# Fixed expert regions, and routing of three batches inside the attention loop

## The reference, cut to what matters

```
c   = bi_wkv(x, f, f, w1, u1, t)           # gate 1: scans over time, per channel
x1  = x + attention(c)                     # 16 heads of 128, causal, softmax
x2  = bi_wkv(x1, f, f, w2, u2, t)          # gate 2: sigmoid(x1) times a factor f2 that needs f alone
s   = sigmoid(x2 @ gate_w)                 # 32 experts in 4 groups
    keep 2 groups by their maxima, then the 6 best experts; weights = s / sum(s)
out = x1 + sum_k weights_k * expert_k(x2) + (silu(x2 @ sw_gate) * (x2 @ sw_up)) @ sw_down
```

## Time and profile before

| | us |
|---|---|
| median of 3 runs | 2662.51 (2656.43 to 2663.44) |
| the profiled execution | 2666.88 |
| its span, first to last instruction | 2664.7 |
| mean granted clock of TensorE | 0.927 |

### The profile page before, as it was taken

One profiled execution on the slowest core, in us unless ns is written; L12 is line 12 of the kernel. 1 busy time (PEld: TensorE's weight loads), 2 busy tenths in 40 slices (PEclk: granted clock), 3 DMA queues, 4 the chain that ended last, 5 costly groups with the idle time before them and its releaser, 6 DMA issues. The chain is left out here.

```text
span 2664.7 us, 41295 instructions
## 1 busy us (share of the span) xinstructions
PE 2283.1 (86%) x11897; PEld 1923.5 (72%) x11899; DVE 1200.3 (45%) x1953; ACT 1123.1 (42%) x2440; POOL 1425.9 (54%) x993
## 2 busy tenths in 40 slices
PE   1558999999999999998379649999999799999676
PEld 1336888788888887777257428999998789999554
DVE  7335777777755555665452002222222122222355
ACT  2226677676766666666221003233333223333211
POOL 5447766766755555454014754444449976520276
PEclk6678999999999999999779759999999899999788
DMA  1445444644464444431423554444446655422366
GB/s 46 123 139 158 141 140 139 198 140 141 137 203 130 129 130 153 116 117 50 171 79 113 214 189 140 146 144 144 131 149 205 210 182 174 152 90 74 112 200 186
DMA packets 284719, 381.97 MB, mean 143 GB/s; under 512 B 19909, under 2 KB 176649, under 8 KB 280649
## 3 DMA queue, kind: packets, MB, share of 16 engines
q1 hardware_dynamic: 230280, 262.16, 32.7%
q10 hardware_dynamic: 38976, 68.17, 7.6%
q0 software_dynamic: 15360, 50.34, 5.9%
HBM read 247.17 MB, written 133.43 MB: 143 GB/s over the span
## 5 line engine op out<-in xcount | busy, mean ns | idle before, releaser
L1585 POOL TENSOR_TENSOR we_low<-we_raw,we_high 128x1408 fp32r<-128x1408 f32 (+1 forms) x96 | 317.7, 3310 | 8.0
L1583 POOL TENSOR_SCALAR we_high<-we_raw 128x1408 fp32r<-128x1408 f32 (+1 forms) x96 | 135.2, 1408 | 320.5 <-PE up_e L365 315.4
L1693 DVE TENSOR_TENSOR hT_low<-hT_ps,hT_high 128x256 fp32r<-128x256 f32 x127 | 54.0, 425 | 390.2 <-ACT hT_high L1659 390.2
L365 PE MATMUL gate_e<-we_high,xT_high 128*128 x508 | 177.8, 350 | 28.2 <-POOL we_low L1585 27.8
L1706 DVE TENSOR_TENSOR hidden_e<-silu_e,up_e 128x352 f32<-128x352 f32 x127 | 66.2, 521 | 293.1 <-ACT silu_e L1670 293.1
L1670 ACT ACTIVATE silu_e<-gate_e 128x352 f32<-128x352 f32 x127 | 59.0, 465 | 326.3 <-PE up_e L365 326.3
L365 PE MATMUL proj<-c_high,wQ_high 128*128 128x512 f32 x256 | 114.0, 446 | 64.6 <-POOL wQ_low L585 64.6
L1675 ACT ACTIVATE rows_out<-down_e 128x512 f32<-128x512 f32 x127 | 76.0, 599 | 216.5 <-PE down_e L365 216.5
L365 PE MATMUL gate_e<-we_high,xT_low 128*128 x508 | 166.2, 327 | 0.0
L365 PE MATMUL gate_e<-we_low,xT_high 128*128 x508 | 165.9, 327 | 0.0
L365 PE MATMUL up_e<-we_high,xT_high 128*128 x508 | 164.2, 323 | 0.0
(11 more groups left out here) (294 smaller groups left out, 7172.6 us busy)
## 6 DMA issues: line engine op xcount, KB each, us to landing
slots_in<-zero_row SPq DMA_DIRECT2D x80, 416.0 KB
rows_in<-slots_in ACTq DMA_DIRECT2D x129, 256.0 KB, 2.8
slots_out<-rows_out ACTq DMA_DIRECT2D x127, 256.0 KB, 2.1
we_raw<-L_ffn_w_gate SPq DMA_DIRECT2D x32, 704.0 KB, 4.5
we_raw<-L_ffn_w_up SPq DMA_DIRECT2D x32, 704.0 KB, 5.1
w_ring<-L_attn_Wq SPq DMA_DIRECT2D x64, 256.0 KB, 3.6
q_T<-q_out SPq DMA_DIRECT2D x64, 256.0 KB, 2.8
w_ring<-L_attn_Wv SPq DMA_DIRECT2D x64, 256.0 KB, 3.7
```

The lines of the kernel that those rows point to most:

```text
L365: last = nc.tensor.matmul(out, a, b, start=start and i == 0, stop=stop and i == len(terms) - 1)
L1583: nc.gpsimd.tensor_scalar(wh[:, p, at:to], raw[:, at:to], 1.0, 1.0, ALU.mult, ALU.mult).then_inc(w_hi, 1)
L1585: nc.gpsimd.tensor_tensor(wl[:, p, at:to], raw[:, at:to], wh[:, p, at:to].bitcast(F32), ALU.subtract).then_inc(w_split, 1)
L1693: nc.vector.tensor_tensor(htl[:, 0:2, :], psh[:, 0:2 * P].rearrange("p (c t) -> p c t", c=2), hth[:, 0:2, :].bitcast(F32), ALU.subtract)
```

## The change

The slot array gets a fixed region of `CAP` = 2048 + 128 rows for each expert, so a token's slot is the expert's region start plus a running count (`cnt`) that is carried from batch to batch. The rows of a batch are scattered once that batch is routed. The stage after attention

- zeroes 128 rows behind each expert's last row: 32 DMAs whose address SP loads from memory, and one for a region of zeros;
- makes a table with the first row of each of the 127 blocks, which ACT reads for every load of the expert stage;
- makes the packed slots that the combination reads, from slot and expert (`final_slots`).

Batches 0 to 2 are cut in 12 chunks of 128 channels (`chunk_of`), two per iteration from iteration 8 on. A chunk is loaded (x1 and f2), goes through a sigmoid and a product, is split in halves, transposed to rows (`T`), gives its part of the logits (`L`) and is stored both as halves (`x2s`) and as rows. Iterations 10, 12 and 14 choose the experts of batch 0, 1 and 2 (`Z`, `choose`), and iterations 10 to 15 scatter two row tiles each (`z0` to `z3` of POOL, 12 indirect DMAs).

Gate 2 now works on the batch of its own iteration and no longer shares keys with gate 1: it has its own key loads, transposes (`Xy`), copy (`hk`), minima (`hm`) and exponentials (`he`). There are 28 key tiles now, 8 more than before; gate 1 is done after iteration 7. The order strings come in three versions: iterations up to 7, 8 to 11, and 12 to 15 (which have no `Q`). The bias of the output projection is added to x when x is stored.

The stage after attention (`last_route_and_shared_up`) routes batch 3 alone, with x1 still on the chip, loads the halves of the other batches, and has no hardware loops. Only its first column piece (4 items, 8 before) goes over POOL. The expert stage begins with four loads of x1 (`xT`) on SP, ahead of the weights.

```diff
-NBLK_ROOM = NBLK + 3
+CAP = T + P
+ZERO_ROW = E * CAP
-PE_ORDER = "S0 V0 V1 V2 a0 Xx S1 b0 V3 Q0 K2 A0 a1 Q1 b1 S2 K3 A1 Q2 S3 a2 k0 b2 Q3 A2 Xk a3 k1 b3 P0 A3 P1 R0 R1 O2 O3".split()
+PE_ORDER = (
...
+    "S0 V0 V1 V2 a0 S1 V3 b0 Q0 Xy A0 T0 L0 K2 a1 Q1 S2 b1 K3 Q2 Z A1 T1 S3 L1 a2 k0 b2 Q3 A2 a3 k1 b3 P0 A3 P1 R0 R1 O2 O3".split(),
...
+def logit_products(nc, out, c, rt, xh, xl, first, last_one):
+    gwh, gwl = rt["gwh"], rt["gwl"]
+    for t in range(TC):
+        ts = slice(t * P, (t + 1) * P)
+        last = split_products(nc, out[:, t * E:(t + 1) * E], [((xh[:, ts], xl[:, ts]), (gwh[:, c, :], gwl[:, c, :]))], first(t), last_one(t))
+    return last
...
+def send_rows(nc, pool, dr, rt, slot, rows, u, part, parts):
+    for k in range(part * TOPK // parts, (part + 1) * TOPK // parts):
+        pool.indirect_dma_start(dr["xs"], bass.IndirectOffsetOnAxis(ap=slot[:, u, k:k + 1], axis=0), rows, None).then_inc(rt["sent"], 16)
...
+            def send(u, part):
+                if part == 0:
+                    pool.wait_ge(slot_done, u // TC + 1)
+                    pool.wait_ge(rows_in, 16 * (u + 1))
+                send_rows(nc, pool, dr, rt, slot, rowt[:].rearrange("p t c -> p (t c)"), u, part, 2)
...
+            def route_sigmoid(j):
+                act.wait_ge(chunk_in, 32 * (j + 1))
+                nc.scalar.activation(rowst[:], rowst[:], ACT.Sigmoid).then_inc(sig_done, 1)
...
+            sp.dma_start(f2[:], dr["f2"][KC * (B - 1):KC * B].rearrange("k p s -> p k s")).then_inc(f2_in, 16)
+            load_shared(0)
+            load_x2(0)
+            load_x2(1)
+            load_shared(1)
+            load_x2(2)
+            sp.dma_start(dr["x1"][B - 1].rearrange("p (k s) -> p k s", k=KC), x1[:]).then_inc(x1_st, 16)
+            load_shared(2)
+            sp.wait_ge(consts, 3)
+            sp.dma_start(dr["xs"][ZERO_ROW:ZERO_ROW + P, :], zero[:]).then_inc(filled, 16)
+            sp.wait_ge(ends_done, 1)
+            for e in range(E):
+                end = sp.value_load(ends[0:1, e:e + 1], min_val=0, max_val=ZERO_ROW - P)
+                sp.dma_start(dr["xs"][bass.ds(end, P), :], zero[:]).then_inc(filled, 16)
+            for m in range(3, len(SCH)):
+                load_shared(m)
...
+            for i, (m, b) in enumerate(items):
+                n, p = SCH[m][1], i % 2
+                if b == 0 and m + 1 < len(SCH):
+                    split_high(m + 1)
+                act.wait_ge(u_mm, i + 1)
+                wait_hidden(act, i - 2)
+                last = nc.scalar.activation(sg[0:n, p, :], psg[p][0:n, :], ACT.Silu)
...
+            for b in range(B):
+                sp.dma_start(xT[:, b, :, :], dr["x1"][b].rearrange("p (k s) -> p k s", k=KC)).then_inc(x1_in, 16)
             with sp.Fori(0, E) as e:
...
             def load(n, p):
-                act.dma_start(xg[:, p, :], dr["xs"][bass.ds(P * n, P), :]).then_inc(xg_in[p], 16)
+                act.dma_start(xg[:, p, :], dr["xs"][bass.ds(row_of(xrow, n, ZERO_ROW), P), :]).then_inc(xg_in[p], 16)
```

More of the change, by code:

```diff
@@ new lines, in projections, with gate_use, x2_transposes @@
+    return seq
+def gate_use(gate, it):
+    return it + NG + (max(it, 0) if gate == 1 else min(it + 1, NFIRST))
+def x2_transposes(nc, out, x2, ident):
+    for t in range(TC):
+        last = nc.tensor.transpose(out[:, t * P:(t + 1) * P], x2[:, t * P:(t + 1) * P], ident[:])
+    return last
+def logit_products(nc, out, c, rt, xh, xl, first, last_one):
+    gwh, gwl = rt["gwh"], rt["gwl"]
+    for t in range(TC):
+        ts = slice(t * P, (t + 1) * P)
+        last = split_products(nc, out[:, t * E:(t + 1) * E], [((xh[:, ts], xl[:, ts]), (gwh[:, c, :], gwl[:, c, :]))], first(t), last_one(t))
+    return last
@@ new lines, in slot_counts @@
+def slot_counts(nc, out, rt):
+    chosen, before, onesb = rt["chosen"], rt["before"], rt["onesb"]
+    w = TC * E
+    nc.tensor.matmul(out[:, 0:w], before[:], chosen[:], start=True, stop=False)
+    for j in range(TC - 1):
+        rest = TC - 1 - j
+        rhs = chosen[:, j * E:(j + 1) * E].unsqueeze(1).broadcast_to([P, rest, E])
+        nc.tensor.matmul(out[:, (j + 1) * E:w], onesb[:], rhs, start=False, stop=j == TC - 2)
+    for j in range(TC):
+        last = nc.tensor.matmul(out[:, w:w + E], onesb[:], chosen[:, j * E:(j + 1) * E], start=j == 0, stop=j == TC - 1)
+    return last
@@ L1316, in _ @@
                     pe.wait_ge(row_done, 1)
-                    nc.tensor.matmul(psl[0:1, 0:P], ebb[:], identb[:], start=True, stop=True).then_inc(row_mm, 1)
+                    pe.wait_ge(left, KC)
+                    for c in range(2):
+                        last = nc.tensor.transpose(pst[0][0:1, c * P:(c + 1) * P], tabf[:, c:c + 1], ident[:])
+                    last.then_inc(row_mm, 1)
         @block.scalar
         def _(act):
-            act.wait_ge(gw_in, 16)
-            nc.scalar.activation(gwh[:], gw[:], ACT.Copy).then_inc(gw_hi, 1)
@@ L1473, in _, with x2_chunk @@
-            then(last)
-            with nc.allow_low_precision(reason="zeros and ones"):
-                red(chosen[:], oh[:].rearrange("p k n -> p n k"), AX.X, ALU.add).then_inc(chosen_done, 1)
-            split_low(1)
-            split_low(2)
-            dve.wait_ge(pos_mm, 1)
-            then(tt(more[:], pslg[:, 0:E].unsqueeze(2).broadcast_to([P, E, NT]), iota_q[:].unsqueeze(1).broadcast_to([P, E, NT]), ALU.is_gt))
+            def x2_chunk(c):
+                dve.wait_ge(sig_done, CHUNKS + c + 1)
+                tt(x2[:, c, :], x2[:, c, :], f2[:, c, :], ALU.mult).then_inc(x2_done, 1)
@@ L1481, in _ @@
+            then(nc.vector.scalar_tensor_tensor(out=count[:], in0=iota_e[:], scalar=-float(CAP), in1=cnt[:], op0=ALU.mult, op1=ALU.add))
+            then(tt(more[:], count[:].unsqueeze(2).broadcast_to([P, E, NT]), iota_q[:].unsqueeze(1).broadcast_to([P, E, NT]), ALU.is_gt))
             then(red(nb[:], more[:], AX.X, ALU.add))
```

1014 lines of the change are left out of this document (570 added, 444 removed).

## The result

The changed kernel took 2710.89 us (median of four runs, 2704.22 to 2714.16), the kernel before beside it 2662.98 (2656.43 to 2666.48): ratio 1.0185, 95% interval 1.0168 to 1.0202. Forecast were 2588 us; it came out 48 us slower instead of 74.5 faster. The profiled execution took 2714.16 us with a span of 2712.2.

What follows compares the result with a forecast made beforehand. PE was taken as the bound in attention and experts, the stage between as poor. Attention +26, that stage -114 and experts +13.5 gave -74.5 from 2662.5: 2588 us, range about 2545 to 2640.

Steps and rivals of the forecast that it cites:

- Iterations -5 to 7: Attention: second key transposes in eight iterations and a new order, +7 us, bounds -6 and +24.
- Iterations 8 to 11: Attention: chunk transposes and logits on full PE, +18 us (16 to 27); ACT's table changes, +4 (0 to +17).
- Iterations 12 to 15: Attention: added PE work fills the 4 to 5 us of waits each, 0 us, bounds -10 and +14.
- x1 store gone: End of attention: batch 3's x1 stays on the chip, so the awaited store moves, -4.4 us.
- The stage behind: Stage after attention: 183 us against 297, -114, bounds -130 and -85.
- the 75 us: Old stage after attention: time lost beside 76 scatters; by the skill's rule on taken branches, straight-line code has none.
- Experts: Expert stage: four x1 loads ahead of the first weights, first product 28 us in instead of 14.7, +13.5 us.
- Scatters starving PE: Rival, attention: 72 scatters cost 70 us, total 2658, or 2623 at a half; chance 0.12, a third at full price.
- Table changes: Rival, attention: 28 ACT table changes of 1.28 us in the chain, 36 us, total 2620; chance 0.09.
- POOL blocking: Rival, iterations 10 to 15: scatters paid in full, 15.4 us each, 92 us, total 2680; chance 0.04.
- The fills held: Stage after attention: fills delay queued weights, PE stands some 20 us; rival without this hold, 2568 us, chance 0.13.

Runs made afterwards that it cites:

- f2_store_early: Changed kernel with SP's store of `g_nb` (f2) issued ahead of the last ring load, at the end of its own iteration; ratio 1.0043 to the kernel before.
- before_store_late: Kernel before with the store of `g_nb` moved behind the key rows, zero fill and first ring load of the next iteration; ratio 1.0155.
- f2_before_c_load: f2_store_early with the store of `g_nb` also ahead of the 2 MB of c loads at a batch's end; ratio 1.0053 to the kernel before.
- The ladder: Single executions of a repaired changed kernel, cutting scatters, then choice, then chunk work; iterations 8 to 14: 5, 30 and 64 us for these.
- mended_no_choice: Changed kernel with store, sigmoid and late loads reordered, without attention's scatters and choice of experts and slots; iteration 9 took 74.8 us.
- mended_no_routing: mended_no_choice also without the chunks' loads, sigmoids, halves, transposes, logits and stores; iterations 8 to 14 2.5 us faster than the kernel before.
- late_stage_loads: choice_in_pieces with weights of pieces 3 to 5 loaded before and among the fills, x1 loads behind two experts' weights; ratio 1.0035 to the kernel before.
- choice_in_pieces: f2_before_c_load with first-chunk work behind `b0` and `K2`, second-chunk work later, counts' bank returned early, slots computed in four pieces; ratio 1.0146 to the kernel before.
- before_straight_line: Kernel before with the four hardware loops over the shared-up items' batches written out, POOL's scatters still in their loop; ratio 0.9959.

## Why the prediction was wrong

- **Iterations -5 to 7, +7 with bounds -6 and +24: failed; it was +43.** The work beside PE was sized right (PE 66.95 us in f2_store_early's iteration 5 against 66.70 before, and DVE's 51.48 hid it). What failed is the sentence "The order is new, and 1.4 us an iteration were waits before". I let busy time bound the effect of a new order. One store behind one ring load cost 38 us in iterations 1 to 7. f2_store_early takes it away, before_store_late makes it in the old kernel (41 us). With the store ahead of the c loads too (f2_before_c_load), iterations 1 to 7 take 475.5 us against 478.3 before: the work added there cost nothing. Both orders could be read beforehand.
- **Iterations 8 to 11, +18 and +4: failed; it was +60.** The PE term was right: iteration 9 has 70.10 us against 65.91, 4.2 forecast. But "PE is full, so all that it gets is paid" holds only while nothing else stops it. ACT's table changes, at 4 us in this term, were worth 13.6 in it (20.4 over the whole of attention); 29.1 us of waits at V2 in iterations 8 to 11 came with a sigmoid queued behind a load, and a lower clock followed. I had written that the first one stands "ahead of the exponentials of head 0, and behind a chunk load", and priced it at 1 us an iteration: the wait has a source and a length (a store of 4.4 us alone, a reload, a chunk), and I didn't add them up.
- **Iterations 12 to 15, 0: failed; 12 to 14 were +52.** The idle time of before is not room. The added work came in chains (DVE's choice, then `k_low`, `pT_low`, the bank) that made new waits instead of filling the old. The ladder shows it for all seven iterations: 64 us for the chunks, 30 for the choice, where PE's own work for the chunks is 4.2 an iteration, 25. Iteration 9 takes 74.8 us in mended_no_choice and 66.3 in mended_no_routing: 4.2 of the 8.5 are PE's work, about 2.5 the lower clock (0.95), and under 2 waits.
- **x1 store gone, -4.4: right.** From V0 of iteration 15 to the end, 57.8 instead of 62.2 us.
- **The stage behind, 183: right (184.1), in part by luck.** The first item came 22.7 us in (27 forecast), and the wait for piece 3, ahead of item 10, was 23.4 us (20 forecast): the two errors cancel. The 32 fills were issued in 44.4 us (45 forecast), but the last ten, which come after the scatters, still stand 1.09 us apart, so their pace there is not the scatters'. I had taken SP's `TENSOR_LOAD` ahead of each fill as small; no run separates it. The cause of the 75 us was read wrongly: the loops were 21 of them, POOL's chain was through only 3 us before the items, and ACT's lateness beside the scatters stays in straight-line code. The sum held because the changed stage has 24 scatters instead of 96, and its items run evenly beside them.
- **Experts +13.5: it was +9.1.** The first `gate_e` came 25.4 us in, not 28. late_stage_loads gives these back.
- **Together:** 42.7 us in iterations -5 to 7, 59.9 in 8 to 11, 51.7 in 12 to 14 and -4.4 at the end are the 150 of attention.
- **Rivals.** Scatters starving PE: 28 us to the end of attention, of the 70 of the rival, and 5 in another order. Table changes: 20 of 36. POOL blocking: not in the changed kernel, but it turned up in choice_in_pieces. The fills held. None of the rivals was a wait that the new order makes between queues: SP's store and DVE's scan, 37 us of the 124 that attention came out above the forecast, and a sigmoid behind a load.
- **The chance of 0.04 for slower** came from that: all rivals had one mechanism in the added work, none in what was merely rearranged.

**Two rules beside it.** The Trainium skill ("DMA: Bandwidth & Descriptors", Queues, rings and completion order) says that each DMA engine takes a ring's descriptors in order. The rows above agree: with 2 MB of c loads ahead, the store issued at 503.16 holds the scan until 511.27; issued ahead of them at 499.91, it lets the scan start at 502.83.

The Trainium skill ("Runtime: NRT & Kernel Launch", Instruction fetch mechanics) was cited for the stage's term. By it straight-line code has no stalls from taken branches. In before_straight_line the items end 21 us earlier, which fits, but waits of 1 to 1.7 us with the releaser "issue" stay inside the products, as at 1529.61 (1.67 us), beside the scatters, and ACT's idle time of 27.09 us ("remote") stays too. What they are is open.

## What to carry to other kernels

When a change rewrites an order, the busy time of the bound engine says nothing on the waits that the order makes. Take each in-order queue at an iteration's border and write behind every waiting instruction what it waits for, how long that takes from its own source, and what stands behind it: a store of a buffer that is soon overwritten goes first, an instruction whose input comes back through DRAM goes last. An engine that was held up runs its queue in one burst afterwards; look at what the other engines do beside it. And before a poor stage is priced by its slowest engine, follow who ends it: idle time there belongs to another queue.
